# The last expert layer in 17 tiles of 128 features, its sums in PSUM, the shares multiplied in by Pool

## What is computed

```
def _silu_and_mul(gu, inter):
    return jax.nn.silu(gu[..., :inter]) * gu[..., inter:]
logits = x @ W_router.T
probs = jax.nn.softmax(logits.astype(jnp.float32), axis=-1)
rw, sel = jax.lax.top_k(probs, TOP_K)                      # TOP_K = 2 of 8
combine = jnp.zeros((T, E), x.dtype).at[jnp.arange(T)[:, None], sel].add(rw)
sh = _silu_and_mul(x @ Ws_gate_up, 704) @ Ws_down
shared_out = sh * jax.nn.sigmoid(x @ W_sgate.T)
gu = jnp.einsum('th,ehi->eti', x, We_gate_up)              # eight experts of 176 features
eo = jnp.einsum('eti,eih->eth', _silu_and_mul(gu, 176), We_down)
return shared_out + jnp.einsum('eth,te->th', eo, combine)
```

## Time and profile before

| | us |
|---|---|
| median of 3 runs | 4503.33 (4503.21 to 4511.71) |
| profiled execution, its own time | 4508.96 |
| its span | 4507.1 |
| layer norm of L3_ffn begins | 4206.03 |
| first matmul of the experts | 4251.74 |
| last matmul ends | 4501.51 |

### The profile page before, as it was taken

One profiled execution on the slowest core, in us unless ns is written; L12 is line 12 of the kernel. 1 busy time (PEld: TensorE's weight loads), 2 busy tenths in 40 slices (PEclk: granted clock), 3 DMA queues, 4 the chain that ended last, 5 costly groups with the idle time before them and its releaser, 6 DMA issues. The chain is left out here.

```text
span 4507.1 us, 45082 instructions
## 1 busy us (share of the span) xinstructions
PE 3448.3 (77%) x17494; PEld 2469.2 (55%) x17494; DVE 2302.8 (51%) x4062; ACT 1167.9 (26%) x2400; POOL 761.3 (17%) x508
## 2 busy tenths in 40 slices
PE   3788953454999988589689679769599766599799
PEld 2676842211334555478479469559455564455455
DVE  3323446787335543745745744754435465255333
ACT  3002210143004531223223324314135311045211
POOL 0000020011005841000000000000048500068200
PEclk8556555566999988789879879869789886699899
DMA  1000000001000011000000000000200000200200
GB/s 32 0 1 13 1 27 0 2 0 57 13 0 1 1 39 64 14 4 1 0 5 1 0 5 1 1 5 1 66 1 1 29 14 0 66 1 1 59 0 10
DMA packets 60224, 60.44 MB, mean 13 GB/s; under 512 B 16669, under 2 KB 55885, under 8 KB 59437
## 3 DMA queue, kind: packets, MB, share of 16 engines
q1 hardware_dynamic: 58989, 56.12, 4.3%
q0 software_dynamic: 1024, 1.45, 0.1%
HBM read 56.51 MB, written 1.05 MB: 13 GB/s over the span
## 5 line engine op out<-in xcount | busy, mean ns | idle before, releaser
L1683 POOL TENSOR_SCALAR work<-work,small 128x512 f32<-128x512 f32 x384 | 594.1, 1565 | 1135.2 <-DVE small L1619 1135.2
L2713 ACT ACTIVATE work<-psum 128x512 f32<-128x512 f32 x384 | 229.3, 597 | 464.4 <-PE psum L2658 237.7
L1614 DVE TENSOR_REDUCE small<-psum 128x2 f32<-128x1024 f32 x192 | 234.9, 1225 | 179.2 <-PE psum L1564 179.2
L1661 ACT ACTIVATE work<-psum,small 128x512 f32<-128x512 f32 x384 | 260.6, 683 | 251.9 <-DVE small L1614 251.9
L2692 DVE TENSOR_TENSOR work<-psum,work 128x256 f32<-128x256 f32 x320 | 136.0, 425 | 282.8 <-PE psum L2649 277.6
L2658 PE MATMUL psum<-work 128*128 128x128 f32 x1280 | 247.5, 275 | 0.0
L2656 PE MATMUL psum<-work 128*128 128x128 f32 x1280 | 247.5, 275 | 0.0
L1574 PEld LDWEIGHTS psum<-consts,work 128*128 128x128 f32 x1536 | 165.9, 141 | 113.5 <-issue 102.4
L1564 PE MATMUL psum<-keysT,arena_a 64*128 64x512 f32 x768 | 218.9, 648 | 9.2 <-ACT work L1661 6.2
L1586 PE MATMUL psum<-work,keys 128*64 128x256 f32 x1536 | 187.0, 384 | 37.1 <-issue 34.2
L1574 PE MATMUL psum<-consts,work 128*128 128x128 f32 x1536 | 211.8, 281 | 3.1 <-DVE work L1625 2.6
(11 more groups left out here) (541 smaller groups left out, 6889.4 us busy)
## 6 DMA issues: line engine op xcount, KB each, us to landing
arena_a<-in_L_xattn_Wo SPq DMA_DIRECT2D x3, 2048.0 KB, 12.5
arena_a<-in_L_xattn_Wq SPq DMA_DIRECT2D x3, 2048.0 KB, 15.2
arena_a<-in_L_xattn_w_kc_q SPq DMA_DIRECT2D x3, 1536.0 KB, 19.8
arena_a<-in_L_attn_w_qkv SPq DMA_DIRECT2D x1, 4096.0 KB, 14.4
arena_b<-in_L_ffn_We_gate_up SPq DMA_DIRECT2D x1, 2816.0 KB
arena_a<-in_L_xattn_W_qr SPq DMA_DIRECT2D x3, 768.0 KB, 4.4
arena_b<-in_L_ffn_w_fc SPq DMA_DIRECT2D x1, 2048.0 KB, 8.1
arena_b<-in_L_ffn_w_proj SPq DMA_DIRECT2D x1, 2048.0 KB, 13.0
```

The lines of the kernel that those rows point to most:

```text
L1614: nc.vector.tensor_reduce(top[:, 2 * u:2 * u + 2], ps[:, u % 2 * 2:u % 2 * 2 + 2, :], AX.X, ALU.max, negate=True).then_inc(*maxed.up())
L1661: nc.scalar.activation(probs[u % NPB][:, j, :], ps[:, u % 2 * 2 + j, :], ACT.Exp, bias=top[:, i:i + 1], accum_out=total[:, i:i + 1]).then_ ...
L1683: nc.gpsimd.tensor_scalar(probs[u % NPB][:, j, :], probs[u % NPB][:, j, :], total[:, i:i + 1], None, ALU.mult).then_inc(*scaled.up())
L2713: nc.scalar.activation(tsb[j].rearrange("p c f t -> p (c f t)"), ps[:, j, :], ACT.Copy).then_inc(*tcopy.up())
```

## The change

The stage is written anew; nothing ahead of its layer norm changes.

- `l3_ffn_weights` lays out one tensor `gu` of all 2112 gate and up columns side by side, and `down` of all 2112 rows. Its 25 transfers are issued by SP inside the block of the layer norm.
- `l3_ffn` is one block. The router's eight columns and the shared expert's one are a single set of 16 matmuls. The features go in 17 tiles, 16 of 128 and one of 64, across the borders of the experts. `hidden(i)` is two groups of four matmuls, `output(i)` eight matmuls, two tiles after, which all add to the same four PSUM banks from the first tile to the last. DVE adds them to x once, at the end.
- As a tile can hold rows of two experts, the share is multiplied in before the sum. The shares are turned (8 transposes), copied by ACT, written to a scratch tensor in DRAM, and read back so that each partition of a feature holds the 1024 shares of its expert: `common` for the shared expert's tiles 0 to 4, three buffers `share` in turn for the tiles from 5 on. POOL multiplies the activated gate by this, DVE then by the up half.
- x is copied out in four parts, each after its own addition.

```diff
-def layernorm(k, interleave=False):
+def layernorm(k, interleave=False, fetch=None):
...
+        if fetch:
+            @block.sync
+            def _(sp):
+                fetch(sp)
...
+def l3_ffn_weights(k):
+
+    io, A, A2, W = k.io, k.arena_b, k.arena_a, k.work
+    A.reset(), A2.reset(), W.reset()
+    E, F, SH = 8, 176, 704
+    w_r, before, after = W.take(P, 2, 9), W.take(P, 64), W.take(P, 64)
+    gu, down = A.take(P, 2, 2, SH + E * F), A2.take(P, 17, D)
+    k.held = w_r, before, after, gu, down
+
+    def fetch(sp):
+        with k.nc.allow_non_contiguous_dma(reason="router columns side by side"):
+            load(k, sp, "l3f_r", [(w_r[:, :, 0:8], rows(io["L3_ffn_W_router"])), (w_r[:, :, 8:9], rows(io["L3_ffn_W_sgate"])),
+                                  (before, k.const("before")), (after, k.const("after"))])
+        shared = io["L3_ffn_Ws_gate_up"].rearrange("(c p) (z n) -> p c z n", p=P, z=2)
+        for name, a, b in (("l3f_a", 0, 256), ("l3f_b", 256, SH)):
+            load(k, sp, name, [(gu[:, c, z, a:b], shared[:, c, z, a:b]) for c in range(2) for z in range(2)])
+            if a == 0:
+                load(k, sp, "l3f_d", [(down[:, 0:5, :], rows(io["L3_ffn_Ws_down"][0:640, :])),
+                                      (down[0:64, 5, :], io["L3_ffn_Ws_down"][640:SH, :])])
+        own = io["L3_ffn_We_gate_up"].rearrange("e (c p) (z n) -> p c z e n", p=P, z=2)
+        for name, a, b in (("l3f_e", 0, 3), ("l3f_f", 3, E)):
+            load(k, sp, name, [(gu[:, c, z, SH + a * F:SH + b * F].rearrange("p (e n) -> p e n", n=F), own[:, c, z, a:b])
+                               for c in range(2) for z in range(2)])
+            if a == 0:
+                own_down = io["L3_ffn_We_down"].rearrange("e n d -> (e n) d")
+                load(k, sp, "l3f_d", [(down[64:P, 5, :], own_down[0:64, :]),
+                                      (down[:, 6:16, :], rows(own_down[64:64 + 1280, :])),
+                                      (down[0:64, 16, :], own_down[64 + 1280:, :])])
+    return fetch
...
 def l3_ffn(k):
-    w_r, w_s, before, after = A.take(P, 2, E), A.take(P, 2, 1), A.take(P, 64), A.take(P, 64)
-    we, wed = A.take(P, E, 2, 2 * 176), A.take(FP, E, RT, D)
-    ws, wsd = A2.take(P, 2, 2 * 704), A2.take(FP, SH, D)
-    weights = A.take(P, NT, 16)
-    hT = [A2.take(FP, 2, N) for _ in range(2)]
-    silu = [W.take(FP, 512) for _ in range(4)]
-    tmp = W.take(P, 1280)
...
-            load(k, sp, "l3f", [(ws, rows(io["L3_ffn_Ws_gate_up"])), (wsd, rows(io["L3_ffn_Ws_down"], FP)),
-                                (we, io["L3_ffn_We_gate_up"].rearrange("e (c p) d -> p e c d", p=P)),
-                                (wed, io["L3_ffn_We_down"].rearrange("e (c p) d -> p e c d", p=FP))])
...
-    route(k, w_r, before, after, weights[:, :, 1:9], tmp, "l3f_r", over_all=True)
+    TILES, LAG, NH = 17, 2, 4
+    h = [A2.take(P, 2, 512) for _ in range(NH)]
+    silu = [A2.take(P, 512) for _ in range(4)]
+    share = [A2.take(P, 2, 512) for _ in range(3)]
+    common = W.take(P, 2, 512)
+    raw, weights, weightsT, tmp = W.take(P, NT, 9), W.take(P, NT, 9), W.take(9, 2, 512), W.take(P, 1280)
+    scratch = k.nc.dram_tensor("l3_shares", (9, N), F32, kind="Internal").ap()
...
+    def width(i):
+        return P if i < TILES - 1 else 64
+
+    def pieces(i):
+        first, last = i * P, i * P + width(i)
+        cuts = [first] + [c for c in range(SH, last, F) if first < c] + [last]
+        return [(a - first, b - first, (a - SH) // F) for a, b in zip(cuts, cuts[1:]) if a >= SH]
...
+            k.wait_weights(pe, "l3f_r")
-                    mm = nc.tensor.matmul(ps[:, 0, t:t + 1], xnT[:, c, t * P:(t + 1) * P], w_s[:, c, :],
+                    mm = nc.tensor.matmul(ps[:, 0, t * 9:(t + 1) * 9], xnT[:, c, t * P:(t + 1) * P], w_r[:, c, :],
...
-    units = [(0, ws, 704, 2 * u, wsd[:, 2 * u:2 * u + 2]) for u in range(SH // 2)]
-    units += [(1 + e, we[:, e], 176, 0, wed[:, e]) for e in range(E)]
...
+            def hidden(i):
+                n_f = width(i)
+                for name, first in (("l3f_a", 0), ("l3f_b", 2), ("l3f_e", 5), ("l3f_f", 9)):
+                    if i == first:
+                        k.wait_weights(pe, name)
+                for n in range(2):
+                    g = 2 * i + n
                     if g >= 2:
                         pe.wait_ge(*hid.at(g - 1))
                     for z in range(2):
-                        col = z * width + (f0 + f) * FP
                         for c in range(2):
-                            mm = nc.tensor.matmul(ps[0:FP, g % 2 * 2 + z, :], w[:, c, col:col + FP],
+                            mm = nc.tensor.matmul(ps[0:n_f, 4 + g % 2 * 2 + z, :], gu[:, c, z, i * P:i * P + n_f],
                                                   xnT[:, c, n * 512:(n + 1) * 512], start=c == 0, stop=c == 1)
                     mm.then_inc(*up.up())
-            def output(u):
-                wd = units[u][4]
-                pe.wait_ge(*hid.at(4 * u + 4))
+            def turn():
+                pe.wait_ge(*weighed.at(1))
+                pe.wait_ge(*gated.at(1))
                 for t in range(NT):
-                    g = NT * u + t
-                    if g >= 4:
-                        pe.wait_ge(*added.at(g - 3))
-                    for f in range(2):
-                        mm = nc.tensor.matmul(ps[:, 4 + g % 4, 0:D], hT[u % 2][:, f, t * P:(t + 1) * P], wd[:, f, :],
-                                              start=f == 0, stop=f == 1)
-                    mm.then_inc(*down.up())
-
-            for u in range(len(units) + 1):
-                if u < len(units):
-                    hidden(u)
-                if u >= 1:
-                    output(u - 1)
+                    mm = nc.tensor.transpose(ps[0:9, 1 + t // 4, t % 4 * P:(t % 4 + 1) * P], weights[:, t, :], k.c["ident"])
+                mm.then_inc(*turned.up())
+
+            def output(i):
+                n_f = width(i)
+                if i == 0:
+                    k.wait_weights(pe, "l3f_d")
+                    pe.wait_ge(*kept.at(2))
+                pe.wait_ge(*hid.at(2 * i + 2))
+                for t in range(NT):
+                    mm = nc.tensor.matmul(ps[:, t // 2, t % 2 * D:(t % 2 + 1) * D],
+                                          h[i % NH][0:n_f, t // 4, t % 4 * P:(t % 4 + 1) * P], down[0:n_f, i, :],
+                                          start=i == 0 and t % 2 == 0, stop=i == TILES - 1, skip_group_check=True)
+                    if t % 2 == 1:
+                        mm.then_inc(*summed.up())
+
+            for i in range(TILES + LAG):
+                if i < TILES:
+                    hidden(i)
+                if i == 0:
+                    turn()
+                if i >= LAG:
+                    output(i - LAG)
...
+            def product(g):
+                i, n = divmod(g, 2)
+                n_f = width(i)
+                dve.wait_ge(*scaled.at(g + 1))
+                if i >= NH and n == 0:
+                    dve.wait_ge(*summed.at(4 * (i - NH + 1)))
+                nc.vector.tensor_tensor(h[i % NH][0:n_f, n, :], silu[g % 4][0:n_f, :], ps[0:n_f, 4 + g % 2 * 2 + 1, :],
+                                        ALU.mult).then_inc(*hid.up())
+
+            for g in range(2 * TILES):
+                product(g)
+            for q in range(4):
+                dve.wait_ge(*summed.at(4 * (TILES - 1) + q + 1))
+                nc.vector.tensor_tensor(x[:, 2 * q:2 * q + 2, :], x[:, 2 * q:2 * q + 2, :],
+                                        ps[:, q, :].rearrange("p (t d) -> p t d", t=2), ALU.add).then_inc(*added.up())
...
+            for g in range(2 * TILES):
+                activate(g)
+                if g == 0:
+                    act.wait_ge(*turned.at(1))
+                    for n in range(2):
+                        nc.scalar.activation(weightsT[:, n, :], ps[0:9, 1 + n, :], ACT.Copy).then_inc(*kept.up())
+
+        @block.gpsimd
+        def _(pool):
+            for g in range(2 * TILES):
+                i, n = divmod(g, 2)
+                n_f = width(i)
+                if g == 0:
+                    pool.wait_ge(*shared_in.at(16))
+                if i >= 5 and n == 0:
+                    pool.wait_ge(*k.sig(f"share_{i % 3}").at(arrive_count(i)))
+                pool.wait_ge(*silud.at(g + 1))
+                own = common if i < 5 else share[i % 3]
+                nc.gpsimd.tensor_tensor(silu[g % 4][0:n_f, :], silu[g % 4][0:n_f, :], own[0:n_f, n, :], ALU.mult).then_inc(*scaled.up())
+
+        @block.sync
+        def _(sp):
+            sp.wait_ge(*kept.at(2))
+            sp.dma_start(scratch, weightsT.rearrange("p a b -> p (a b)")).then_inc(*stored.up(16))
+            sp.wait_ge(*stored.at(16))
+            row = lambda e, n: scratch[e:e + 1, :].broadcast_to([n, N])
+            sp.dma_start(common.rearrange("p a b -> p (a b)"), row(0, P)).then_inc(*shared_in.up(16))
+            for i in range(5, TILES):
+                if i >= 8:
```

(62 more changed lines are left out.)

66 lines of the change are left out of this document (15 added, 51 removed).

## The result

The changed kernel's median is 4426.7 us (4421.77 to 4427.78, 4 runs), against 4506.26 us for the kernel before (4503.21 to 4511.71, 4 runs). The ratio is 0.982, with a 95% interval from 0.9803 to 0.9837: 1.8% faster; the medians lie 79.6 us apart. The forecast was 4419.8 with a range from 4410 to 4435.

What follows compares the result with a forecast made beforehand. TensorE's matmuls were taken to bound the last stage. Fewer matmuls 72.3, head 9.3 and tail 1.9 sum to 83.5 us, which from a median of 4503.33 gives 4419.8 us, range 4410 to 4435.

Steps and rivals of the forecast that it cites:

- What bounds the kernel: In the last stage, from 4251.74 us on, only TensorE's matmuls: time is their number and their price.
- Fewer matmuls: In the stage's stream, 136 matmuls of each kind instead of 192, at 0.859 and 0.432 us each: 72.3 us less.
- SP's held issues: In the head, the layer norm's block ends only when SP has issued all 25 transfers, taken as 4221.5 us.
- Rival A: In the head, the fetch holds the layer norm's block 11.2 us longer, at 219 GB/s: 4431.0 us; chance 0.12.
- the first tile: In the head, its `hidden` takes 6.87 us and 2.0 for the cold clock, beside DVE's chain, until 4237.9 us.
- the transposes: In the head, eight transposes of the shares at the router's 0.22 us a record: 1.7 us.
- The shares' way: In the head, ACT's copies, a 1.9 us store to DRAM and a 4.4 us read, every microsecond counting in full.
- rival B: In the head, 128 partitions reading one DRAM row take 15 us instead of 4.4, once: 4430.4 us; chance 0.09.
- Pool: Its multiplication by the share takes 1.04 us, by the row of L1825.
- The steady state: In the stream, PE's 5.16 us a group covers Pool's step; end to product 2.5 us; from 5.16 us Pool sets the pace.
- The head as a whole: Before the stream, PE goes on at 4249.3 us with one tile's `hidden` already done: 9.3 us gained.
- The tail: From PE's end to the span's end, 3.7 us instead of 5.59: 1.9 us gained.

Runs made afterwards that it cites:

- e2: Changed kernel with 24 tiles of 88 features instead of 17 of 128, second matrices and shares in 88 partitions: 4507.3 us, stage 300.85 us.
- e5: Changed kernel with Pool multiplying the activated gate by itself instead of by the share: stage 220.6 us against 219.7.
- e3: Changed kernel with each Pool multiplication preceded by one more of the same form into a spare buffer: 4427.13 us, stage 223.6 us.
- e4: Changed kernel with each Pool multiplication preceded by four more of the same form: 4481.97 us, stage 280.3 us.
- e8: Changed kernel with the share multiplied in after VectorE's product and the experts' own weights fetched one block later: 4403.97 us, ratio 0.9769 to the kernel before.
- e1: Changed kernel with its 25 weight transfers put back into a block of their own behind the layer norm: 4434.55 us, stage 229.8 us.
- e7: Changed kernel with 14 transfers issued in the layer norm's block, the experts' own 11 at the start of the next: 4413.19 us, stage 211.6 us.

## Why the prediction was right, and where its terms were off

**What bounds the kernel**: right. The stream is PE from end to end, before and after.

**Fewer matmuls**, 72.3 us: right, and shown by e2, where 72.4 come back. In the changed kernel itself the term is 71.1. Two small things eat 1.2. The last tile has 64 features and doesn't cost the same as the others, as the prediction had it, but more: its `hidden` is 7.01 us instead of 6.87, and the last three `output` 10.77 instead of 3 x 3.45. And tiles 1 and 2 took 2.64 us more than at full clock, where 2.0 were allowed. No surcharge for 128 columns was right.

**SP's held issues**, last return 15.5 us into the stage: too little by 3.3, the largest miss. It was 18.75, with 268 x 18.75 = 5.03 MB of the 6.56 MB landed, 77%. The prediction had bounds of 45% and 84% from two cases and took a point between them, for no reason but that the last transfers are small. The rate it took, 306 GB/s, was about right for the whole (268 with the slow start, 329 to 346 once running). The new list's shape was nearer to L1_xattn's, nearly all to 128 partitions, and its 84% the better row. Rival A's reason was read too widely: of the 6.56 MB before only the second matrices, 2.1 MB, went through 88 partitions. e2 shows that these alone are enough to hold the router back by 8.1 us.

**The router** (6.97 us), **the first tile** (8.41 against 8.9) and **the transposes** (0.89 against 1.7): the last was priced by the router's record at the low clock, and ran at the full one (1.00 in 4234 to 4236 us).

**The shares' way**: ACT 1.07, store 1.80, read 4.10, against 1.3, 2.0 and 4.4 with their waits. The rival B (15 us for the read) is out: one DRAM row for 128 partitions took 3.5 to 4.2 us in all runs with 128 partitions. By the Trainium skill's page "DMA: Bandwidth & Descriptors", section "Anatomy of one DMA — SWDGE (gpsimd) path", the two would have been 2.1 and 3.2, an estimate. The rows here are under it for the store and over it for the read; these transfers were issued by SP, which is not what that section describes, and the row of a transfer of the same size was the nearer guide.

**Pool**, 1.04 us: 1.27, which costs 0.2 us once, in the head, and nothing in the stream. The step that failed is the choice of the row: L1825 squares a tensor, and e5 shows that reading the same tensor twice is what makes it 1.04. The trace of before has rows of Pool with two different inputs, for twice the elements, and the forecast did not use them. They stand in that of after as well:

```profile
L2701 POOL TENSOR_TENSOR arena_b<-arena_b,work 128x1024 f32<-128x1024 f32 x16 | 36.9, 2340 | 262.6 <-DVEq L72 262.6
```

Half of 2.34 us is 1.17, nearer to 1.27 than 1.04 is. The steady state's claims held: a group's end to its product is 2.7 us instead of 2.5, at the tightest there are 3.43, and e3 and e4 bear out both the cover and the turning point at 5.16 us. Nor did Pool and VectorE hinder each other. In the changed kernel VectorE's product mostly starts when Pool's has ended, but in e4, where Pool goes on with its next multiplication beside every product of VectorE, they take 1.26 and 0.69 us, as they do here. That agrees with what the prediction cited of the page "SBUF — State Buffer", section "Who interferes with whom", of the Trainium skill.

**The head as a whole**: 44.60 us to PE's resumption instead of 43.3; a gain of 8.0 instead of 9.3. Of the 3.2 us by which the router came late 1.9 were paid back by the transposes, the first tile and the transfers. **The tail**: 3.3 instead of 3.7.

So the forecast came out 2.1 us off in the stage, by errors of both signs that happened to offset each other; the single misses are up to 3.3 us. The median lies 6.9 us above it: 2.9 because the forecast started from 4503.33 us, and the kernel before has 4506.26 with one run more; the other 3.9 are 83.5 less the 79.6 us between the two medians, of which the stage shows 2.1 and the spread of the runs covers the rest.

**What the prediction did not ask** is whether the two waits that it priced, SP's held issues and the way through DRAM, have to stand on PE's path. e8 takes 21 us out of them (its other 1.7 are the clock's).

## What to carry to other kernels

When a transfer's issues are moved under other work, ask what else the issuing engine's block holds up. Here only what the next block needs first belonged in the layer norm's block, and the rest cost nothing one block later. When a per-column factor arrives late, put its multiplication behind the step that makes PSUM free, so that the late value is waited for by work that comes much later. Where the same columns are streamed in any case, fill all 128 weight columns and rows: seven tiles fewer were worth 71 of the 81 us.

## What the runs showed of the hardware that was not expected

- Pool multiplies two different 128x512 fp32 tensors in 1.27 us and one by itself in 1.04 (e5), with all else equal.
- The first tile of large matmuls behind the router's small ones took 8.37 to 10.00 us in nine executions of 16 records (e2's with 88 weight columns; 6.87 at full clock; the shortest two 8.37 in e1 and 8.41 in after, the longest 10.00 in e5). Differences below 2 us between single executions of this stage are therefore no evidence.
- After PE had gone idle at about 4209.3 us its granted clock was still 1.00 in 4210 to 4212 us, and 0.54 in the next window. In e8 matmuls of nine columns that started 1.05 us after the layer norm's last ones began at the full clock, and did not hold it; in e7, after the same gap, they began at 0.50.
- A fetch whose second matrices go to 88 partitions moved 224 GB/s in 4217 to 4231.5 us (e2), one without such loads 329 to 346 in 4210 to 4214 us (after), at DMA shares of 0.99 and of 1.11 to 1.17. By the order of issue over half of the bytes in e2's window are still of loads to 128 partitions. A load to 88 partitions by itself stands at the end of the fetch of before, whose last transfer is 1.4 MB of second matrices; by the order of issue this window holds nothing else, and it moved 134 GB/s:

```profile
4238.00:4246.00 8.00, 1.73 (x9) 1.76 (x9) 5.69 (x24) 1.36 (x2) 0.00 (x0) 0.50 0.76 134
```

  By the Trainium skill's page "DMA: Bandwidth & Descriptors", section "Why a DMA increments its semaphore by 16 and not by 1", a transfer is spread over the largest number of engines up to 16 that divides the slowest dimension of both its sides, which is 11 for 88 partitions; 11/16 of 329 to 346 is 226 to 238 GB/s, an estimate for such a load by itself. The 134 GB/s measured are far under it, so the number of engines is not shown to be the cause, and no run here shows which engines a transfer used. The cause stays open.
- A last tile of 64 features took 0.14 us more in `hidden`, and the last three `output` with it 0.4 more, than full ones. No run here shows why.
